# Two layers of attention and experts on one core: attention 1 without a barrier between its pairs, attention 2 entered batch by batch, two clearing blocks dropped

## The chip, the core and the metric

One core of a Trainium2 chip runs the whole program. The metric is the device time in microseconds, taken as the median of several runs.
## What is computed

`x` has 4 batches of 512 tokens, 256 wide, float32. Each of the four steps is a residual of the layer norm of `x`:

```python
x = x + attention_1(layernorm(x))        # one head, softmax(QK^T/16) V W_o inside each batch
x = x + experts_1(layernorm(x))          # 12 experts, top 3, 256 -> 640 -> 256, relu
x = x + attention_2(layernorm(x))        # 16 heads of 16, against 4096 given keys and values
x = x + experts_2(layernorm(x))          # 8 experts, top 2, and a shared one
```

Inside `experts_1` a token's result is the sum over its 3 experts, plus a bias row. That result of a whole batch is averaged over its tokens and goes through a small network, `phi = sigmoid(relu(pooled @ Wp1 + bp1) @ Wp2 + bp2)`; where `phi > 0.7` the batch's result is multiplied by 0.2. So a batch's `x` isn't known before all its expert rows are summed and averaged over tokens. For exactness attention 2 takes each row's maximum over 4096 scores before the exponentials.

## The kernel before

All of `x` stays in SBUF as 16 tiles of 128 tokens (4 a batch). There is no planner around the change: each engine's order is the order of its code in a block.

**Attention 1** (lines 314 to 518) works on two batches at a time, `lanes` one and two, each with 4 of the 8 PSUM banks and its own buffers. A `nc.Fori` loop of two rounds holds one block: layer norm 0 of both lanes (`norm_vector` on DVE, the power on POOL, transposes `norm_tensor` on PE, copies `norm_scalar` on ACT), `qkv`, `scores`, `turn_probs`, `weigh`, `output`, then `x` is updated (L506), layer norm 1, its rows written to DRAM (`normed_rows`, L350), and `router` (L429) gives the 12 logits. Each round ends with the block's end and `clear(...)` (L518), a second block in which the engines set 52 semaphores back to zero, since the loop body waits on constants.

**Experts 1** (to L927): routing on DVE, then 59 blocks of 128 token slots. Each block's result is written by POOL to the DRAM tensor `expert_rows`, by slot and expert rank. When all are written, SP reloads them (L644), 12 DMAs of 512 KB, 3 for each of the 4 batches, into the space of the second expert weights. DVE adds the three of a batch to `acc` (L922), and PE sums over tokens (L754). Then the block ends, and `clear` (L927) is a block again.

**Attention 2, first part** (L1072 to L1257) is one block. DVE works out all four batches' factors together (L1207 to L1221), updates batch 0's `x` (L1231) and normalises it; POOL updates the others (L1149, L1151). PE makes queries (`half_queries`, L1077), which are split in two float32r parts, written to DRAM (`store_queries`, L1102) and loaded back in the layout of the score products (`load_queries`, L1020). SP issues the loads of all keys first (L1003: the first quarter of the keys, then the rest), and batch 0's query store after them. Then come 64 units: PE makes a unit's scores (2 products of 128x512, L1042, `max_unit`) in one of two bank pairs, DVE reduces it to maxima (L1048). Unit `u` has query tile `u//16`, key block `u%16//2` and head pair `u%2`; the units from 4 on wait for the rest of the keys. Among the units `PIECE`, `STATS` and `APPLY` place the layer norm and the queries of batches 1 to 3, which PE does in lumps of half a batch. The next block (L1336) has the exponentials and weighted sums of attention 2, with further units among them.

Of the kernel before, what the change touches and what calls it, by code (L numbers as in the profile page):

```python
# [5 lines left out]
F32 = mybir.dt.float32  # L6
# [9 lines left out]
P = 128  # L16
# [36 lines left out]
def build(nc, a, out):  # L53
    with ExitStack() as ctx:
# [81 lines left out]
        class Lane:  # L136
            def __init__(self, tag, bank, xn, xnT, stack):
# [5 lines left out]
                self.stats_done, self.aggr_done, self.var_done, self.rstd_done, self.norm_done, self.turned, self.taken = self.norm_sems = (  # L143
                    [sem(n + tag) for n in ("ln_stats", "ln_aggr", "ln_var", "ln_rstd", "ln_norm", "ln_turned", "ln_taken")])
# [42 lines left out]
        main = Lane("", 0, xn, xnT, ctx)  # L187
# [44 lines left out]

        with ExitStack() as l0:
# [78 lines left out]

            with ExitStack() as at:
                scale = float(D) ** -0.5

                class AttnLane(Lane):
                    def __init__(self, c):
                        tag = str(c)
                        xn_, xnT_ = (xn, xnT) if c == 0 else (sb("xn1", [P, TB, D], F32, at), sb("xnT1", [P, KD, S], F32, at))  # L320
                        super().__init__(tag, 4 * c, xn_, xnT_, at)
# [5 lines left out]
                        self.nmax, self.rsum, self.rrec = (sb(n + tag, [P, TB], F32, at) for n in ("nmax", "rsum", "rrec"))  # L327
                        (self.q_mm, self.k_mm, self.v_mm, self.score_mm, self.pT_mm, self.pv_mm, self.proj_mm, self.route_mm,
                         self.q_taken, self.k_taken, self.v_taken, self.nmax_done, self.p_done, self.pT_act, self.pT_dve,
                         self.o_taken, self.rrec_done, self.x_done, self.rows_out) = self.attn_sems = sems(" ".join(n + tag for n in (  # L330
                             "q_mm k_mm v_mm score_mm pT_mm pv_mm proj_mm route_mm q_taken k_taken v_taken nmax_done "
                             "p_done pT_act pT_dve o_taken rrec_done x_done rows_out").split()))

                lanes = [AttnLane(c) for c in range(2)]
                assert NB % 2 == 0

                with nc.Fori(0, NB // 2) as b2i:
                    def rows_of(c):
                        return lambda t: x[:, bass.ds(2 * TB * b2i + TB * c + t, 1), :].rearrange("p o d -> p (o d)")

                    with nc.Block() as block:
                        @block.sync
                        def _(sp):
                            for j in range(E0 // 2):
                                e = bass.ds(E0 // 2 * b2i + j, 1)
                                sp.dma_start(w2all[:, e].rearrange("p o n d -> p (o n) d"),
                                             a["L0_ffn_w2"][e].rearrange("o (k p) i -> p (o k) i", p=P)).then_inc(w2_in, 16)
                            for c, L in enumerate(lanes):
                                sp.wait_ge(L.norm_done, 2 * TB)
                                sp.dma_start(normed.rearrange("(t p) d -> p t d", p=P)[:, bass.ds(2 * TB * b2i + TB * c, TB), :],  # L350
                                             L.xn[:]).then_inc(L.rows_out, 16)
                            for L in lanes:
                                sp.wait_ge(L.rows_out, 16)

                        @block.gpsimd
                        def _(pool):
                            for L in lanes:
                                norm_pool(pool, 0, L)
                            for L in lanes:
                                norm_pool(pool, 1, L)  # L360
                        @block.tensor
                        def _(pe):
                            def project(L, w, bank, done):
                                for m in range(KD):
                                    for k in range(KD):
                                        mm = nc.tensor.matmul(ps[:, bank + m, :], w[:, k, m * P:(m + 1) * P], L.xnT[:, k, :],
                                                              start=(k == 0), stop=(k == KD - 1))
                                    mm.then_inc(done, 1)

                            def qkv(L):  # L370
                                B = L.bank
                                pe.wait_ge(L.taken, KD)
                                pe.wait_ge(qkv_in, 16 * 3)
                                project(L, wq, B + 2, L.q_mm)
                                project(L, wk, B, L.k_mm)
                                for i in range(TB):
                                    if i % 2 == 0:
                                        pe.wait_ge(L.q_taken, i // 2 + 1)
                                    for k in range(KD):
                                        mm = nc.tensor.matmul(ps[:, B + 2 + i // 2, (i % 2) * D:(i % 2 + 1) * D],  # L380
                                                              L.xnT[:, k, i * P:(i + 1) * P], wv[:, k, :],
                                                              start=(k == 0), stop=(k == KD - 1))
                                    if i % 2:
                                        mm.then_inc(L.v_mm, 1)

                            def scores(L):

                                pe.wait_ge(L.k_taken, KD)
                                for i in range(TB):
                                    if i >= 2:  # L390
                                        pe.wait_ge(L.v_taken, i - 1)
                                    for m in range(KD):
                                        mm = nc.tensor.matmul(ps[:, L.bank + i, :], L.qT[:, m, i * P:(i + 1) * P], L.kT[:, m, :],
                                                              start=(m == 0), stop=(m == KD - 1))
                                    mm.then_inc(L.score_mm, 1)

                            def turn_probs(L):
                                pe.wait_ge(L.p_done, TB)
                                for kb in range(TB):
                                    for i in range(TB):  # L400
                                        mm = nc.tensor.transpose(ps[:, L.bank + kb, i * P:(i + 1) * P],
                                                                 L.pm[:, i, kb * P:(kb + 1) * P], ident[:])
                                    mm.then_inc(L.pT_mm, 1)

# [1733 lines left out]
```

## Time and profile before

| | us |
|---|---|
| median of 3 runs (lowest, highest) | 2159.94 (2159.7, 2162.9) |
| the profiled execution's own time | 2163.98 |
| its span, first to last instruction | 2162.3 |
| PE busy in the span | 1972.8 (91%) |
| DVE busy | 1555.3 (72%) |
| ACT busy | 1345.0 (62%) |
| POOL busy | 272.0 (13%) |

Durations below come from the one profiled execution, whose own time is 4.0 us above the median. In the timeline a row is: start in us, length in us, engine, line, operation, output<-inputs, count; in brackets how long the engine had been idle before and what ended that. PE ends are modelled. "PEq" or "issue" as a releaser stands for an engine's instruction queue, at block borders for the meeting of all engines.

### The profile page before, as it was taken

How to read it: one execution, taken by the hardware profiler on the slowest of the kernel's cores; microseconds unless marked ns; L12 is line 12 of the kernel's file. 1: busy time of each engine (PE TensorE's matmuls, PEld its weight loads, DVE VectorE, ACT ScalarE, POOL GpSimd, SP SyncE). 2: the span in 40 equal slices, each digit the busy share in tenths (PEclk: the TensorE clock that was granted, in tenths of full speed). 3: DMA queues.
4: the chain of work that ended last, by engine and by line, in shares of the span. 5: the costliest groups of instructions: out<-in, count | busy, mean ns of one | idle time of the engine just before them, and what ended most of it. 6: DMA issues, size and time to landing. Idle time of an engine off the chain costs nothing. (4 is left out here: it accounts for less than half of the span.)

```text
span 2162.3 us, 40151 instructions
## 1 busy us (share of the span) xinstructions
PE 1972.8 (91%) x15900; PEld 996.3 (46%) x15900; DVE 1555.3 (72%) x1956; ACT 1345.0 (62%) x2647; POOL 272.0 (13%) x280
## 2 busy tenths in 40 slices
PE   6793999996477999999999999999999999998995
PEld 3553889996222333333333333333333333446673
DVE  3436212223488999999999999999999999613454
ACT  1220444441012888888888888888888888784321
POOL 0000434431310000000000000000000000001473
PEclk9896899997566999999999999999999999999997
DMA  4201668874552311011310003201102000001135
GB/s 145 73 20 61 200 211 254 262 232 158 88 73 50 45 18 17 7 19 30 51 19 15 14 12 49 43 8 15 19 7 86 5 7 7 12 25 37 40 102 167
DMA packets 162028, 145.92 MB, mean 67 GB/s; under 512 B 85322, under 2 KB 132406, under 8 KB 161078
## 3 DMA queue, kind: packets, MB, share of 16 engines
q1 hardware_dynamic: 152438, 117.69, 22.2%
q0 software_dynamic: 9408, 25.70, 3.7%
q8 instruction: 126, 2.06, 0.4%
q14 instruction: 56, 0.46, 0.1%
HBM read 108.63 MB, written 32.10 MB: 65 GB/s over the span
## 5 line engine op out<-in xcount | busy, mean ns | idle before, releaser
L1048 DVE TENSOR_REDUCE maxp<-banks 128x2 f32<-128x1024 f32 x1024 | 1233.8, 1223 | 35.2 <-PE banks L1042 34.4
L1525 ACT ACTIVATE pring<-banks 128x512 f32<-128x512 f32 x2048 | 1107.3, 601 | 185.2 <-PE banks L1412 64.5
L1426 PE MATMUL banks<-pring,vcur 128*17 128x256 f32 x8192 | 637.9, 386 | 4.9 <-ACT osb L1519 4.0
L1412 PE MATMUL banks<-qst,kst 50*128 50x512 f32 x2048 | 510.9, 496 | 0.0
L1042 PE MATMUL banks<-kst,qst 50*128 50x512 f32 x2048 | 431.4, 419 | 28.3 <-DVE maxp L1048 25.5
L1412 PEld LDWEIGHTS banks<-qst,kst 50*128 50x128 f32 x2048 | 193.6, 184 | 425.8 <-ACT pring L1525 413.0
L1426 PEld LDWEIGHTS banks<-pring,vcur 128*17 128x17 f32 x8192 | 139.7, 95 | 370.5 <-issue 185.9
L1042 PEld LDWEIGHTS banks<-kst,qst 50*128 50x128 f32 x2048 | 199.7, 192 | 66.5 <-DVE maxp L1048 54.5
L773 ACT ACTIVATE hT<-banks,b 128x128 f32<-128x128 f32 x295 | 108.5, 368 | 187.8 <-PE banks L704 172.7
L911 DVE TENSOR_SCALAR yo<-banks,wblock 128x256 f32<-128x256 f32 x59 | 28.5, 483 | 224.5 <-PE banks L713 224.5
L1394 POOL TENSOR_TENSOR osb<-osb,bc 128x512 f32<-128x512 f32 x15 | 19.2, 1282 | 1169.2 <-DMA bc<-reciprocals 1169.2
L704 PE MATMUL banks<-xgT,w1r 128*128 128x128 f32 x1180 | 143.8, 278 | 1.0 <-issue 1.0
L704 PEld LDWEIGHTS banks<-xgT,w1r 128*128 128x128 f32 x1180 | 138.8, 195 | 1.4 <-issue 1.4
L713 PE MATMUL banks<-w2all,hT 128*128 x590 | 137.8, 381 | 0.0
L713 PEld LDWEIGHTS banks<-w2all,hT 128*128 128x128 f32 x590 | 107.6, 190 | 15.0 <-issue 2.7
L174 ACT COPY xnT<-banks 128x512 f32<-128x512 f32 x24 | 12.9, 589 | 109.9 <-PE banks L179 109.9
L657 POOL DMA_INDIRECT expert_rows<-yo,target_i x59 | 61.3, 1039 | 157.6 <-DVE yo L911 152.6
L179 PE MATMUL banks<-ident,xn 128*128 128x128 f32 x96 | 23.3, 387 | 63.3 <-DVE xn L160 42.9
L1822 PE MATMUL banks<-wgu,xgT 128*128 x156 | 52.5, 459 | 0.0
L169 POOL TENSOR_TENSOR rstd<-vareps,mhalf 128x4 f32<-128x4 f32 x16 | 16.2, 1016 | 260.7 <-DVE vareps L153 260.7
L179 PEld LDWEIGHTS banks<-ident,xn 128*128 128x128 f32 x96 | 14.5, 188 | 71.8 <-DVE xn L160 45.6
L2059 DVE COPY xgT<-banks 128x256 f32<-128x256 f32 x39 | 16.6, 425 | 36.7 <-PE banks L1835 36.7
(294 smaller groups left out, 1287.0 us busy)
## 6 DMA issues: line engine op xcount, KB each, us to landing
w1r<-in_L_ffn_w SPq DMA_DIRECT2D x59, 640.0 KB
kst<-key_parts SPq DMA_DIRECT2D x18, 512.0 KB
key_parts<-ksp SPq DMA_DIRECT2D x32, 256.0 KB, 3.4
w2all<-in_L_ffn_w SPq DMA_DIRECT2D x12, 640.0 KB, 7.5
w2all<-expert_rows SPq DMA_DIRECT2D x12, 512.0 KB, 8.7
qst<-query_parts SPq DMA_DIRECT2D x96, 64.0 KB
normed_rows<-xn SPq DMA_DIRECT2D x8, 512.0 KB, 2.9
kf<-in_kT SPq DMA_DIRECT2D x16, 256.0 KB, 5.7
```

Source lines behind the costliest of these rows:

```text
L179: mm = nc.tensor.transpose(ps[:, L.bank + k, t * P:(t + 1) * P], L.xn[:, t, k * P:(k + 1) * P], ident[:])
L657: nc.gpsimd.indirect_dma_start(placed, bass.IndirectOffsetOnAxis(ap=target_i[:, b:b + 1], axis=0), yo[b % YO][:], None).then_inc(y_out[b % ...
L704: mm = nc.tensor.matmul(ps[:, HB + n % HR, 0:P], w1r[b % W1R][:, k, i * P:(i + 1) * P], xgT[b % 2][:, k, :], start=(k == 0), stop=(k == KD ...
L713: mm = nc.tensor.matmul(ps[:, YB + b % 2, 0:D], hT[b % 2][:, i, :], w2all[:, bass.ds(e, 1), i, :].rearrange("p o d -> p (o d)"), start=(i ...
L773: nc.scalar.activation(hT[b % 2][:, i, :], ps[:, HB + n % HR, 0:P], ACT.Relu, bias=b1[:, bass.ds(e * NI + i, 1)]).then_inc(h_taken, 1)
L911: nc.vector.tensor_scalar(yo[b % YO][:], ps[:, YB + b % 2, 0:D], wblock[:, b:b + 1], None, ALU.mult).then_inc(y_taken, 1)
L1042: mm = nc.tensor.matmul(ps[:, base + r, :], qst[i][rows, hp, qt * P:(qt + 1) * P], keys[rows, hp, kb * 512:(kb + 1) * 512], start=True, st ...
L1048: return nc.vector.tensor_reduce(maxp[:, :, hp, qt, kb], ps[:, base:base + 2, :], X, ALU.max)
L1412: nc.tensor.matmul(ps[:, score_bank(n), :], kst[g % 2][rows, j // 2, kt * P:(kt + 1) * P], qst[i][rows, j // 2, :], start=True, stop=True) ...
L1426: mm = nc.tensor.matmul(ps[32 * j:32 * j + VC, 7, cols], vcur[g % 2][:, kt, j, :], pring[:, (G % 2) * HG + j, cols], start=(kt == 0 and ha ...
L1525: nc.scalar.activation(pring[:, n % (2 * HG), :], ps[:, score_bank(n), :], ACT.Exp, scale=float(DH) ** -0.5).then_inc(exp_done, 1)
L1822: mm = nc.tensor.matmul(ps[:, bank, 0:2 * H1], xgT[b % 2][:, k, :], wgu[:, k, bass.ds(experts[b], 1)].rearrange("p o g h -> p (o g h)"), s ...
```

## The change

It has three parts.

**Attention 1.** The loop is written out, in one block, and semaphores count on instead of being cleared. The second layer norm of a lane is an object of its own, `L.late`, whose rows and transposes lie in the lane's probabilities `pm`. The second pair's first layer norm is placed before the first pair's `add_result`; the first pair's transposes (`turn_late`) and router products come after the second pair's `qkv`.

**Clearing.** `clear` is no longer called after attention 1 and after experts 1. ACT sets attention 1's 68 semaphores back in the experts' block, after its second exponential, and the experts' 29 in attention 2's first block.

**Attention 2, first part.** The expert rows are reloaded in this block, batch 0's three DMAs first, then the first quarter of the keys, then batches 1 to 3, into `kst[1]`, `pring` and a new buffer. DVE adds batch 0's and 1's rows, POOL 2's and 3's. The factor is worked out for batch 0, for batch 1, and for 2 and 3 together among the units. The rest of the keys is loaded after batch 0's queries, and units go by key block first, so that only those from 16 on need it. POOL normalises batches 1 to 3. PE makes queries in single pieces of two instructions, and the token sums of batches 2 and 3 at units 2 to 5 and 8 to 11.

```diff
-                with nc.Fori(0, NB // 2) as b2i:
-                    with nc.Block() as block:
-                    clear(*[s for L in lanes for s in L.norm_sems + L.attn_sems])
+                with nc.Block() as block:
...
+                        for it in range(PAIRS_OF_BATCHES):          # PE
+                            qkv(one, it)
+                            qkv(two, it)
+                            if it:
+                                for L in lanes:
+                                    turn_late(L, it - 1)
+                                for L in lanes:
+                                    router(L, it - 1)
+                            scores(one, it)
+                            scores(two, it)
+                            turn_probs(one, it)
+                            turn_probs(two, it)
+                            weigh(one, it, 0)
+                            weigh(one, it, 1)
+                            weigh(two, it, 0)
+                            output(one, it)
+                            weigh(two, it, 1)
+                            if it + 1 < PAIRS_OF_BATCHES:
+                                norm_tensor(pe, it + 1, one)
+                            output(two, it)
+                            if it + 1 < PAIRS_OF_BATCHES:
+                                norm_tensor(pe, it + 1, two)
...
+                            if it + 1 < PAIRS_OF_BATCHES:           # DVE, after the softmax sums
+                                dve.wait_ge(x_loaded[1], 16)
+                                for c, L in enumerate(lanes):
+                                    norm_vector(dve, it + 1, rows_of(it + 1, c), L)
                             for c, L in enumerate(lanes):
+                                add_result(c, it)
+                                dve.wait_ge(L.pT_mm, TB * (it + 1))
+                                norm_vector(dve, it, rows_of(it, c), L.late)
...
-                clear(step, sums_done, *route0_sems, *fill_sems, *block_sems, *xg_in, *w1_in, *y_out, *sums_in)
...
+                PIECE = {u0 + i if i < TB else u1 + i - TB: (b, i) for b, u0, u1 in ((1, 6, 23), (2, 32, 38), (3, 47, 53))
+                         for i in range(TB + KD * KD)}
+                def first_unit(n):
+                    kb, qt, h = n // 8, n % 8 // 2, n % 2
+                    return 16 * qt + 2 * kb + h
...
+                        load_sums(sp, 0)                            # SP
                         sp.wait_ge(zeros_set, 1)
+                        load_zeros(sp, 0)
                         load_ones(sp, 0, keys_in0)
                         load_keys(sp, 0, 0, keys_in0, slice(0, FEW))
+                        for c in range(1, NB):
+                            load_sums(sp, c)
+                        store_half(sp, 0, 0)
+                        sp.wait_ge(q_stored, 16)
+                        load_query_parts(sp, 0, 0)
                         load_keys(sp, 0, 0, keys_in1, slice(FEW, KEYS))
+                        store_half(sp, 0, 1)
...
+                        pow_of(0)                                   # POOL
+                        for n, c in enumerate((2, 3)):
+                            pool.wait_ge(erows_in[c], 16 * TOP0)
+                            for k in range(TOP0):
+                                w = nc.gpsimd.tensor_tensor(acc[:, tiles, :], acc[:, tiles, :], expert_sums[c][:, k], ALU.add)
                         for b in range(1, NB):
+                            pow_of(b)
+                            for t in range(TB * b, TB * (b + 1)):
+                                nc.gpsimd.tensor_scalar(xn[:, t - TB * b, :], x[:, t, :], meanvar[:, t, 0:1], rstd[:, t:t + 1],
+                                                        ALU.subtract, ALU.mult).then_inc(main.norm_done, 1)
+                            for m in range(KD):
+                                leave(pool, b, m)
...
+                        add_rows(0)                                 # DVE
+                        factors(0, 0, 1, 2)
+                        residual(0, 0)
+                        stats_of(0)
+                        (normalise batch 0)
+                        add_rows(1)
                         (split batch 0's queries, as before)
+                        factors(1, 1, 2, 6)
+                        residual(1, 1)
                         stats_of(1)
                         for u in range(NU):
+                            if u in FACTOR:
+                                factor_step(FACTOR[u], 2, 2, NB, POOLED_BANK)
+                            if u in LATE:
+                                residual(LATE[u], 2)
+                                stats_of(LATE[u])
                             dve.wait_ge(max_mm, u + 1)
+                            max_reduce(first_unit(u), 0, 4 + 2 * (u % 2)).then_inc(max_taken, 1)
```

`add_rows` is two additions of 128x1024 and four of 128x256, `factors` the eight steps of L1207 to L1221 for one batch, `residual` one operation of 128x1024. On PE the token sums of batch 0 come before its transposes, those of batch 1 (16 instructions) after batch 0's queries. `FACTOR` puts the eight steps of batches 2 and 3 at units 12 to 25, `LATE` their residual and statistics at 26 and 28.

## Rows read from the trace of the kernel before

**Rows 1.** The page, busy tenths of DVE in 40 slices.
```profile
DVE  3436212223488999999999999999999999613454
```

**Rows 2.** Timeline of PE in attention 1.
```profile
33.67 3.60 PE L366 MATMUL banks<-xnT,wq 128*128 128x512 f32 x8
43.99 13.90 PE L393 MATMUL banks<-kT,qT 128*128 128x512 f32 x32
...
82.87 1.04 PE L179 MATMUL banks<-ident,xn 128*128 128x128 f32 x8
88.84 6.82 PE L429 MATMUL banks<-wr,xnT 128*128 128x12 f32 x32
...
129.39 13.90 PE L393 MATMUL banks<-kT,qT 128*128 128x512 f32 x32
```

**Rows 3.** Timeline of DVE around the two rounds of attention 1.
```profile
73.59 0.88 DVE L506 SCALAR_TENSOR_TENSOR x<-banks,rrec,x 128x256 f32 x2 [11.77 <-PE banks L419]
...
183.35 0.35 DVE L205 TENSOR_REDUCE zmax<-z 128x16 f32<-128x192 f32 x1 [1.87 <-PEq L97]
```

**Rows 4.** Busy times, mean granted clock, DMA share and GB/s: the router products.
```profile
88.84:95.80 6.96, 6.82 (x34) 6.72 (x32) 0.21 (x1) 1.07 (x2) 0.00 (x0) 0.50 0.22 75
```

**Rows 5.** Timeline at a block border without a clearing block.
```profile
675.81 0.21 DVE L1069 STREAM_TRANSPOSE mrows<-mparts 128x32 f32<-128x32 f32 x1
676.31 0.61 SPq L1027 DMA_DIRECT2D maxima<-mrows  x1
```

**Rows 6.** Timelines of SP, DVE and PE from the last expert row to the units.
```profile
513.10 13.83 SPq L644 DMA_DIRECT2D w2all<-expert_rows  x12
521.07 3.74 DVE L922 TENSOR_TENSOR acc<-acc,w2all 128x1024 f32<-128x1024 f32 x3 [10.82 <-DMA w2all<-expert_rows]
543.20 0.17 DVE L1207 TENSOR_SCALAR pooled<-banks 128x8 f32<-128x8 f32 x1 [5.16 <-PEq L97]
546.96 1.67 DVE L1231 SCALAR_TENSOR_TENSOR x<-acc,fac,x 128x256 f32<-128x256 f32 x4
551.85 2.85 DVE L160 TENSOR_SCALAR xn<-x,meanvar,rstd 128x256 f32<-128x256 f32 x4 [1.16 <-POOL rstd L169]
556.81 5.22 PE L1077 MATMUL banks<-xnT,wqt 128*128 128x512 f32 x8 [1.16 <-ACT xnT L174]
560.35 0.69 DVE L1238 CAST qsp<-banks 128x512 fp32r<-128x512 f32 x1 [5.65 <-PE banks L1077]
561.85 0.38 SPq L1102 DMA_DIRECT2D query_parts<-qsp  x1
577.00 1.25 SPq L1020 DMA_DIRECT2D qst<-query_parts  x3
583.80 6.39 DVE L1048 TENSOR_REDUCE maxp<-banks 128x2 f32<-128x1024 f32 x5 [14.29 <-PE banks L1042]
```

**Rows 7.** DMA queue from 554 to 577 (packets, MB, share); landing of the query stores.
```profile
q1 hardware_dynamic: 550, 2.72, 92.5%
...
DMA to landing us min/median/max: 2.8/2.8/15.1
```

**Rows 8.** The line of the unit reductions, 583.8 to 675.08, idle before the first included.
```profile
L1048 DVE TENSOR_REDUCE maxp<-banks 128x2 f32<-128x1024 f32 x64 | 74.2, 1217 | 25.2 <-PE banks L1042 24.4
```

**Rows 9.** Timeline of PE among the units: a transposed tile, a unit, a lump.
```profile
612.87 0.69 PE L179 MATMUL banks<-ident,xn 128*128 128x128 f32 x2
613.49 0.79 PE L1042 MATMUL banks<-kst,qst 50*128 50x512 f32 x2
616.33 3.78 PE L1077 MATMUL banks<-xnT,wqt 128*128 128x512 f32 x4
```

**Rows 10.** POOL's additions (whole span); normalising on DVE beside POOL's work, and alone.
```profile
L1151 POOL TENSOR_TENSOR x<-x,acc 128x1024 f32<-128x1024 f32 x3 | 7.0, 2341 | 0.2
...
552.86 1.20 DVE L160 TENSOR_SCALAR xn<-x,meanvar,rstd 128x256 f32<-128x256 f32 x1
608.25 1.37 DVE L160 TENSOR_SCALAR xn<-x,meanvar,rstd 128x256 f32<-128x256 f32 x4
```

More of the change, by code:

```diff
@@ L582, in build @@
                 GROUPS = TOP0
-                spent = w2all[:].rearrange("p e n d -> p (e n) d")
-                sums = [spent[:, c * TOP0 * TB:(c + 1) * TOP0 * TB].rearrange("p (k t) d -> p k t d", k=TOP0) for c in range(NB)]
                 def key_load(n):
@@ L1167, in _, with pool_tokens @@
[L1167 to L1169 removed]
+                        def pool_tokens(c, i, bank):
+                            if c < 2:
+                                pe.wait_ge(erows_done, TB * c + i + 1)
+                            else:
+                                pe.wait_ge(rows_added, c - 1)
+                            for m in range(KD):
+                                mm = nc.tensor.matmul(ps[:, bank + m, c:c + 1], acc[:, TB * c + i, m * P:(m + 1) * P],
+                                                      ones[:, 0:1], start=(i == 0), stop=(i == TB - 1))
+                            return mm
@@ L1233, in _, with add_rows @@
-                        ch.wait()
-                        stats_of(0)
-                        apply_of(0)
+                        ch = Chain(dve, steps[0])
+                        def add_rows(c):
+                            tiles = slice(TB * c, TB * (c + 1))
+                            dve.wait_ge(erows_in[c], 16 * TOP0)
+                            for k in range(TOP0 - 1):
+                                ch(nc.vector.tensor_tensor(acc[:, tiles, :], acc[:, tiles, :], expert_sums[c][:, k], ALU.add))
+                                ch.wait()
+                            for i in range(TB):
+                                t = TB * c + i
+                                nc.vector.tensor_tensor(acc[:, t, :], acc[:, t, :], expert_sums[c][:, TOP0 - 1, i], ALU.add
+                                                        ).then_inc(erows_done, 1)
@@ new lines, in factors, with residual @@
+                        def factors(n, c0, c1, bank):
+                            for i in range(8):
+                                factor_step(i, n, c0, c1, bank)
+                        def residual(b, n):
+                            tiles = slice(TB * b, TB * (b + 1))
+                            dve.wait_ge(fac_done, n + 1)
+                            ch(nc.vector.scalar_tensor_tensor(out=x[:, tiles, :], in0=acc[:, tiles, :], scalar=fac[:, b:b + 1],
+                                                              in1=x[:, tiles, :], op0=ALU.mult, op1=ALU.add))
+                            ch.wait()
```

595 lines of the change are left out of this document (334 added, 261 removed).

## The prediction, made before the changed kernel was run

> **What bounds the kernel now.** I read the page first, the 40 slices before anything else, then the timelines of the stages that the diff touches, engine by engine, and last the waits inside them. From slice 14 on DVE is at nine tenths or more [rows 1]; that long stretch is the softmax of attention 2 and isn't touched. So the change can only pay in what lies before: attention 1 (to 181.5 us), the border to the experts, and the stretch from the last expert row (513) to the last of the 64 units (675). All of these are serial chains; a microsecond taken off them is a microsecond of the end, since the stage behind starts only when all engines have met.
>
> In attention 1 PE is the chain: it works without a gap up to the second layer norm, and then the second round's scores start at 129.39, 85.40 after the first round's at 43.99 [rows 2]. Between, PE waits for layer norms and runs the router products at the half level, 0.50 [rows 2, 4]. DVE meanwhile had stood idle for 11.77 us ahead of L506 [rows 3].
>
> From 513 on the chain is DMA, DVE, PE, DMA, DVE: reload, additions, factor, normalisation, queries, their way through DRAM, first maximum at 583.80 after 14.29 us of idle DVE [rows 6]. Then DVE is the bound of the units, with 74.2 us of reductions [rows 8].
>
> **Part 1, attention 1.** The second pair's first layer norm moves into the idle 11.77 us of DVE: two lanes at some 4.4 us are 8.9, so it fits and costs nothing; had it not that cover, it would delay L506 by the excess. Its transposes take PE about 0.9 us a lane (8 in 1.04, the last one's tail left out [rows 2]), the first lane's ahead of `output(two)`, where PE waited 0.7 us anyway. The last `output` ended at 82.9, so both lanes are turned at about 84.1. `qkv` of both: 2 x (43.99 - 33.67 = 10.32) = 20.6, to 104.7. The late transposes are 1.8, the wait for ACT's first copy 0.4, to 106.9. The 32 router instructions took 6.82 at 0.50 [rows 2, 4]; PE comes to them now from 80 us of dense work, so I take them at the full level, half of that, 3.4: scores at 110.3. Against 129.39 that is **19.1 us**. If the clock had fallen it would be 15.7; without any wait for ACT 19.5. DVE's late layer norm runs beside `qkv` and ends before the first key copy. The second half of the w2 loads is issued behind the row stores and has a hundred microseconds. The end of the last pair (transposes, router, logits) stays as it was.
>
> **Part 2, clearing.** The border to the experts costs 1.87 us from the last logits to the next DVE work [rows 3]; a border without a clearing block costs 676.31 - 676.02 = 0.3 [rows 5]. So **1.6 us**, between 1 and 1.9. The second clearing lies in part 3's chain. The clears on ACT are 68 and 29 in a row: the old block did 13 an engine inside 1.9 us, so at most 0.15 each, 10 and 4 us, and ACT had nothing to do there for over 30 us either time. Without that idle time they would be on the path in full.
>
> **Part 3a, up to the first unit.** SP reloads from 513.10 as before, and batch 0's three DMAs came first before too: additions from 521.07, no gain. Two of 1.25 and four small ones in 1.67 end at 525.2. The 16 token sums start with the first tile, at 0.22 each at half clock (router rate), so they end at 527.7. The old chain from L1207 to L1231 is 546.96 - 543.20 = 3.76: `x` can be worked on at 531.5. Residual 1.3, statistics 2.0, POOL's power 1.2: 536.0. Normalising took 2.85 beside POOL's work [rows 6]; POOL has now nothing to do yet, and alone it is 1.4 [rows 10]. Then PE turns tiles at half clock (2.5, overlapped by half a microsecond), ACT copies 1.1, queries from about 540.2. From their start to the first DVE split it was 560.35 - 556.81 = 3.5, to the second 5.3: 543.7 and 545.5. The first half is stored at 545.2 (561.85 - 560.35 = 1.5 after).
>
> Is DVE free then, and the queue? Their additions began 4.4 us after one another before, so a batch takes the queue 4.4 us. Ahead of batches 1 to 3 stand now the ones and a quarter of the keys, 0.92 MB at 2.72 MB in 23 us [rows 7], 7.8 us. So batch 1 lands near 535.5, 2 at 540, 3 at 544.5. `add_rows(1)` takes DVE from 537.5 to 541.5: hidden. The store meets an empty queue. Before, it stood behind 3.1 MB of keys, and 15.1 us passed until the loads of 577.00; the median from issue to landing is 2.8 [rows 7]. So: loads from 548.2, landed like the old ones (583.80 minus a unit minus 577.00, less two zero loads) at 552.3. This is what the reordering is worth: about 12 us of DMA and, above, 17 us of three batches that needn't be waited for.
>
> DVE goes on: second half's split to 546.9, batch 1's token sums on PE to 547.3, factor 3.8, residual 1.3, statistics 2.0: first maximum near **554.5**, against 583.80, **29.3 us**. Here DVE, no longer the query loads, is last. Bounds: each of some 12 DVE operations after 540 beside POOL's additions may cost 0 to 0.8 us (1.20 against 1.37 / 4 = 0.34 alone [rows 10]), so 554 to 561.
>
> A rule stands against this. The Trainium skill, SBUF — State Buffer (section Who interferes with whom), says that DVE with two SBUF inputs and a GpSimd operation that reads SBUF exclude each other for a whole instruction. The row beside it disagrees in degree: a DVE operation of 1.20 us began at 552.86 and ended within one of POOL that ran from 552.69 to 555.65. By the rule in full, my sum would lose what the first rival has, by rows.
>
> **Part 3b, the 64 units.** Old: 91.3 from first to last, of it 74.2 reductions, 6.7 layer norm of two batches, 25.2 - 14.3 = 10.9 idle. New: reductions 74.2. The normalising is off DVE (-2.7), residual (2 x 1.3) and eight factor steps (1.6) are on: 8.2 in all. Idle time grows, since PE gets more and in a worse place. At half clock a unit takes PE about 0.73, a turned tile 0.62, a piece 3.71 / 2 = 1.85 [rows 9], and DVE 1.14 a unit. Four pieces in four units make 2.6 each, 1.45 over DVE: 5.8 a batch for batches 2 and 3; for batch 1 the steps of units 23 to 25 and the 3.3 us at unit 26 hide part, 3.9. The lumps before left DVE idle 3.3 a batch, because two of them let the clock rise. Token sums at 0.9 in units 2 to 11: 3. Turned tiles: 0.25 x 8 = 2. Together 20.5. Sum 74.2 + 8.2 + 20.5 = 103, against 91.3: **+11.6**. If the clock rises early (it did within 7 to 10 us of dense PE work), the idle is no more than before and this is +2; if every wait adds, +16. The rest of the keys, 2.36 MB from 551, needs 20 us to 573, and unit 16 is due at 576: hidden by 3 us, and otherwise a wait of its own.
>
> The last maximum comes then at 554.5 + 103 = 657.5 in the old scale, 17.7 earlier. POOL's normalising of batch 1 follows its additions (6 x 2.34 from 540, to 554.5) and ends near 559, before the turned tiles of unit 6.
>
> **Sum.** 19.1 + 1.6 + 29.3 - 11.6 = 38.4 us. From the profiled execution's own 2163.98 this gives 2125.6; that one is 4.0 above the median of 2159.94, so I forecast **2121.5**. Its own range, from the bounds above (gains of 15.7 to 19.5, 1 to 1.9, 23 to 30, costs 2 to 16): a loss of all at once isn't likely, 2111 to 2133.
>
> **Rivals.**
> 1. *POOL and DVE exclude each other.* POOL's six additions of 2.34 us [rows 10] lie from 540 to 554, on just the DVE chain that is last. DVE gets in only between them: factor and residual of batch 1 end when POOL's do, first maximum 558 to 559, and POOL, delayed as well, normalises batch 1 only by 562 to 565, where PE, in order, stands before unit 6. 6 to 10 us: 2129. For it: the stretched rows at 551.85 and 552.86. Against it: none was stretched to the end of POOL's instruction. 17 in 100.
> 2. *The clock comes up early among the units.* PE is loaded densely from unit 2 on, and each stretch of extra work lifts the clock before its end; the idle stays at 11 and the stage costs 2 instead of 11.6: 2112. For it: old second lumps. Against it: stretches of 10 us, as long as the rise took. 15.
> 3. *The queries of batch 0 still wait.* If SP or the rings hold the store until batches 1 to 3 and half of the keys are through, the 12 us come back, and unit 16 waits too: 2136. Against it: by amounts the ring is empty in time. 7.
> 4. *Slower than before: instruction supply.* The written-out attention 1 has every instruction once, with no loop, and a stream must be fetched. One stall of POOL for "issue", 5.0 us at 491, is in the trace. Were PE to stand so at each stage of attention 1 and at each border, from the eighth stall on the gain is gone: 2165. Against it: the rest of the kernel is written out and PE shows no such stall in 2000 us. 3.
> 5. *It doesn't do what it says*: the stages gain, and the softmax starts no sooner because something else (value or query loads of the next block) is last: within 0.2%, 2160. 3.
>
> The forecast keeps 55. Eight in ten lie between **2108 and 2137**. Faster by over 0.2% (4.3 us, about what the measurement can tell): 0.94; within: 0.03; slower: 0.03.
>
> **What would show it.** Scores of the second pair near 110 with the clock at 1.0 in the router; a border of 0.3 us ahead of `zmax`; all routing times earlier by 20.7. From the last expert row to the first unit 41.4 us in place of 70.7; the query store landing in under 4 us; DVE's L1048 with idle time near 20 inside the stage. Wrong would be a DVE operation of over 1.5 us beside POOL, PE waiting for `xn` at unit 6 or for keys at unit 16, and ACT's clears ending later than the first relu.

## The result, and the profile after

The changed kernel took 2128.59 us (median of 4 runs, 2126.09 to 2131.45) against 2160.34 for the kernel before beside it: ratio 0.9851, 95% interval [0.9834, 0.9869], 31.8 us. Forecast were 2121.5 and 38.4. Two further sets of runs gave 0.9851 [0.9837, 0.9864] and 0.9852 [0.9837, 0.9867], so the size is firm and the forecast was some 7 us too good. The profiled execution has its own time of 2126.49 and a span of 2124.7; that of before, 2163.98 and 2162.3. Between these two lie 37.6 us of span, more than between the medians; why, is the last point of the explanation.

The page's rows of DVE's busy tenths, of TensorE's granted clock and the line of the unit reductions over the whole span, where [rows 1] had DVE's:

```profile
DVE  2537112224889999999999999999999999513454
PEclk9995999997568999999999999999999999999997
L1095 DVE TENSOR_REDUCE maxp<-banks 128x2 f32<-128x1024 f32 x1024 | 1235.4, 1224 | 20.9 <-PE banks L1089 19.9
```

The nine tenths begin with slice 13 and are as even as before: the softmax wasn't touched, what is gained lies ahead of it. PE in attention 1 (columns of a timeline: start, busy us, engine, line, operation, count, idle before and who ended it), to be held against [rows 2]:

```profile
104.81 1.91 PE L180 MATMUL banks<-ident,pm 128*128 128x128 f32 x16
107.01 3.74 PE L454 MATMUL banks<-wr,pm 128*128 128x12 f32 x32 [0.29 <-ACT pm L175]
110.60 15.68 PE L411 MATMUL banks<-kT,qT 128*128 128x512 f32 x32
126.11 3.72 PE L419 MATMUL banks<-ident,pm 128*128 128x128 f32 x32
```

The second pair's scores start at 110.60 (forecast 110.3, before 129.39), but they take 15.68 where the same 32 products took 13.90. The windows of the same stretch (window, length, busy PE, granted clock, DMA share, GB/s) name the reason; 0.50 is the lower of the two levels, 1.2 GHz:

```profile
107.01:110.75 3.74, 3.74 (x33) 0.99 0.00 0
111.00:114.00 3.00, 3.00 (x4) 0.50 0.00 0
114.30:128.00 13.70, 13.70 (x45) 1.00 0.01 2
```

Here the router ran at full clock, as I took it; the fall came behind it, in the scores, with PE busy all the time. It is part of the change: all eight profiles with both routers ahead of both scores have such a stretch at 0.50, from 109 to 112 us on, 3.4 us long in four of them and 6.8 us in the other four, where it begins inside the router (4.13 to 4.52 us in place of 3.74). DVE at the border to the experts, where [rows 3] has 1.87:

```profile
164.62 0.21 DVE L532 TENSOR_TENSOR z<-banks,br 128x48 f32<-128x48 f32 x1 [3.21 <-PE banks L454]
165.16 0.35 DVE L206 TENSOR_REDUCE zmax<-z 128x16 f32<-128x192 f32 x1 [0.33 <-PEq L349]
```

Routing starts 18.2 us earlier (forecast 20.7), and the border is 0.33 as read off a border without a clearing block [rows 5]. Then DVE from the last expert row to the first unit, against [rows 6]:

```profile
503.36 2.48 DVE L1344 TENSOR_TENSOR acc<-acc,kst 128x1024 f32<-128x1024 f32 x2 [10.97 <-DMA kst<-expert_rows]
505.88 1.43 DVE L1348 TENSOR_TENSOR acc<-acc,kst 128x256 f32<-128x256 f32 x4
...
518.14 1.38 DVE L1406 TENSOR_SCALAR xn<-x,meanvar,rstd 128x256 f32<-128x256 f32 x4 [1.16 <-POOL rstd L1223]
519.44 4.55 DVE L1344 TENSOR_TENSOR acc<-acc,kst 128x1024 f32<-128x1024 f32 x2
524.03 9.90 DVE L1348 TENSOR_TENSOR acc<-acc,kst 128x256 f32<-128x256 f32 x4
533.85 0.68 DVE L1411 CAST qsp<-banks 128x512 fp32r<-128x512 f32 x1
...
543.49 3.49 DVE L1095 TENSOR_REDUCE maxp<-banks 128x2 f32<-128x1024 f32 x3
```

The same six additions take 3.9 us for batch 0 and 14.4 for batch 1 (12.4 in the two later profiles of this kernel): four small ones of 0.36 each take 2.5 each. A DVE operation of over 1.5 us beside POOL was one of the signs of being wrong that the prediction named. POOL at that time, and the DMA queue behind the split:

```profile
520.57 8.11 POOL L1232 TENSOR_TENSOR acc<-acc,pring 128x1024 f32<-128x1024 f32 x3 [2.46 <-DMA pring<-expert_rows]
528.64 7.49 POOL L1232 TENSOR_TENSOR acc<-acc,last_rows 128x1024 f32<-128x1024 f32 x3
```
```profile
535.34 0.37 SPq L1177 DMA_DIRECT2D query_parts<-qsp  x1
538.09 2.65 SPq L1060 DMA_DIRECT2D qst<-query_parts  x6
```

POOL's six additions take 2.5 to 2.7 us each, and DVE's wait for one each. The store lands in 2.75 us. From the last scatter (492.67; 510.53 before) to the first maximum are 50.8 us where there were 73.3: 22.4 gained of 29.3. Last, the line of the 64 units from 543.4 to 639.4, against [rows 8]:

```profile
L1095 DVE TENSOR_REDUCE maxp<-banks 128x2 f32<-128x1024 f32 x64 | 75.8, 1221 | 12.7 <-PE banks L1089 11.7
```

The stage lasts 95.9 us, 4.6 more than before, where I had added 11.6.

### The profile page after: what moved, and what is told of

Read it like the earlier page. It is cut to its first block and busy times, and to the rows that moved or that the text cites. A ratio compares the mean times of both kernels' runs of the same rounds, so it can differ in the third digit from the quotient of the medians.

```text
span 2124.7 us, 40040 instructions
## 1 busy us (share of the span) xinstructions
PE 1971.0 (93%) x15912; PEld 997.2 (47%) x15912; DVE 1559.4 (73%) x1960; ACT 1343.0 (63%) x2648; POOL 287.5 (14%) x292
## 3 DMA queue, kind: packets, MB, share of 16 engines
q1 hardware_dynamic: 152438, 117.69, 22.4%
## 5 line engine op out<-in xcount | busy, mean ns | idle before, releaser
L1095 DVE TENSOR_REDUCE maxp<-banks 128x2 f32<-128x1024 f32 x1024 | 1235.4, 1224 | 20.9 <-PE banks L1089 19.9
L711 POOL DMA_INDIRECT expert_rows<-yo,target_i x59 | 61.3, 1039 | 158.0 <-DVE yo L960 153.0
L175 ACT COPY xnT<-banks 128x512 f32<-128x512 f32 x16 | 8.6, 589 | 62.5 <-PE banks L180 62.5
L1913 POOL DMA_INDIRECT expert_rows<-yo,target_i x39 | 38.5, 987 | 23.0 <-ACT yo L2095 14.8
L2038 PE MATMUL banks<-wd,hT 88*128 x156 | 40.4, 381 | 1.2 <-DVE hT L2248 1.2
L1907 POOL DMA_INDIRECT xg<-normed_rows,source_i x39 | 38.2, 981 | 11.8 <-issue 9.9
```

The lines of the kernel that those rows point to most:

```text
L711: nc.gpsimd.indirect_dma_start(placed, bass.IndirectOffsetOnAxis(ap=target_i[:, b:b + 1], axis=0), yo[b % YO][:], None).then_inc(y_out[b % ...
L1095: return nc.vector.tensor_reduce(maxp[:, :, hp, qt, kb], ps[:, base:base + 2, :], X, ALU.max)
L2038: mm = nc.tensor.matmul(ps[:, 5 + u % 2, 0:D], hT[u % 2][0:HC, c, :], wd[:, bass.ds(e, 1), c, :].rearrange("p o d -> p (o d)"), start=(c = ...
```

## The experiments

Four kernels ran together, beside the kernel before (2162.19 us there).

**The changed kernel again.**

> The changed kernel itself, timed again beside the kernel before, as the reference for the other runs on this chip. If the 31.8 us measured so far are the change's own, the median difference is 31 to 33 us; if the two groups of its four runs (2126 and 2131) are two phases of the clock that a run falls into, both groups come again, and in the profile the stretch to 640 us is the same in either, with the difference behind it.

2131.7 us (2126.43 to 2133.06), ratio 0.9851. The stretch to 640 was not the same: here the first maximum stands at 542.47, a microsecond earlier than in the first profile, and the last ends at 642.55, 3.2 later. So the expected split into two groups, equal up to 640, is not what came: the runs lie between 2126 and 2133 us, and the difference is made inside the units as well as behind them.

**The clearing blocks put back.**

> The changed kernel with its two clearing blocks put back (behind attention 1, and behind the expert block, with ScalarE's clearing inside the blocks taken out). Theory: each costs one barrier round: z to zmax goes from 0.33 back to about 1.9 us of idle, and the expert border gains 1 to 1.5 us, so 2 to 3 us slower than the changed kernel. Rival: the second one is hidden behind the last scatter's landing (VectorE waits 10.97 us for the reloaded rows anyway), then only 1.5 us.

```
+                clear(*attn1_used)          # behind attention 1
-                        for s in attn1_used:
-                            act.sem_clear(s)
-                        for s in block0_used:
-                            act.sem_clear(s)
+                clear(*block0_used)         # behind the expert block
```

2134.3 us (2133.03 to 2137.51), ratio 0.9868 [0.9853, 0.9883] against 0.9851 [0.9837, 0.9864]: about 3.7 us slower, 2.6 between the medians, and the intervals overlap, so that the times alone don't settle it. Its rows at the two borders:

```profile
168.14 0.35 DVE L206 TENSOR_REDUCE zmax<-z 128x16 f32<-128x192 f32 x1 [2.06 <-PEq L97]
...
499.73 0.14 POOL L1215 MEMSET zeros<- 2x64 f32 x1 [4.05 <-POOLq L97]
```

2.06 against 0.33, and 4.05 against 2.77 in the changed kernel: 1.7 and 1.3. The second isn't hidden: the reload is issued after the border, so DVE's wait for it moves along. From the last scatter (494.71) to the first addition (506.73) this kernel takes 12.0 us, the changed kernel 10.6 to 10.7.

**POOL's additions left out.**

> GpSimd's six additions of the expert rows of batches 2 and 3 are left out (those rows are not added; all signals remain). Lock theory (VectorE and GpSimd exclude each other for a whole instruction where both read two operands from SBUF): VectorE's additions of batch 1 fall from 14.4 us to the 3.9 that the same six take for batch 0, the first maximum starts at about 535 instead of 543.5, and the kernel is 8 to 9 us faster than the changed one. Rival (VectorE is slow there because the rows are still landing, or the store and reload of the queries are the bound): the additions stay above 10 us, or the first maximum stays within 1.5 us of 543.5.

```
-                                w = nc.gpsimd.tensor_tensor(acc[:, tiles, :], acc[:, tiles, :], expert_sums[c][:, k], ALU.add)
+                            nc.gpsimd.memset(pool_spare[:, n:n + 1], 0.0).then_inc(rows_added, 1)
```

DVE in this kernel:

```profile
521.62 2.48 DVE L1340 TENSOR_TENSOR acc<-acc,kst 128x1024 f32<-128x1024 f32 x2
524.14 1.43 DVE L1344 TENSOR_TENSOR acc<-acc,kst 128x256 f32<-128x256 f32 x4
527.75 0.69 DVE L1407 CAST qsp<-banks 128x512 fp32r<-128x512 f32 x1 [2.17 <-PE banks L1155]
...
530.66 0.69 DVE L1407 CAST qsp<-banks 128x512 fp32r<-128x512 f32 x1 [1.50 <-PE banks L1155]
```

With nothing on POOL the additions of batch 1 take 3.9 us, exactly those of batch 0, though the same rows are loaded: the lock theory holds, and the rival of late rows falls. Of the 10.5 us only 5 to 7 arrive at the first maximum (33.3 us behind the first addition; 40.1, 38.2 and 38.1 in the three profiles of the changed kernel), since DVE now waits for the queries, which PE computes at half clock (8 products in 6.70 us), 2.17 and 1.50. Median 2126.54 (2125.64 to 2129.44), 5.2 under the changed kernel's 2131.7, where 8 to 9 were expected.

**Router and scores lane by lane.**

> TensorE in attention 1's second pair: router of lane one, scores of lane one, router of lane two, scores of lane two, in place of both routers ahead of both scores; VectorE takes the logits of lane two behind the row maxima of lane one. Theory (the granted clock fell to 0.50 at 111 to 114 us because 16 transposes and 32 narrow products stood in one stretch): with half of them together the clock stays up, the scores take 13.9 us again and the pair ends 1.8 us earlier. Rival (the dip is a late answer to the idle time ahead of it, or any such group is enough): the dip stays, no change within 0.5 us, or it comes twice.

```
-                                for L in lanes:
-                                    router(L, it - 1)
-                            scores(one, it)
-                            scores(two, it)
+                            for L in lanes:
+                                if it:
+                                    router(L, it - 1)
+                                scores(L, it)
```

PE, and the windows:

```profile
107.01 1.96 PE L454 MATMUL banks<-wr,pm 128*128 128x12 f32 x16 [0.29 <-ACT pm L175]
108.82 7.11 PE L411 MATMUL banks<-kT,qT 128*128 128x512 f32 x16
115.77 1.85 PE L454 MATMUL banks<-wr,pm 128*128 128x12 f32 x16
117.47 7.11 PE L411 MATMUL banks<-kT,qT 128*128 128x512 f32 x16
```
```profile
107.01:109.00 1.99, 1.99 (x17) 1.00 0.00 0
111.00:114.00 3.00, 3.00 (x8) 1.00 0.01 3
```

No fall, and the last logits at 162.72 in place of 164.62: 1.9 us, as the theory had it. The median is 2128.9 (2125.66 to 2132.48), inside the changed kernel's range. But this is one profile. Four later ones have the same order; in one of them the clock stays up too, in three it falls again for 3.4 us, as in the kernel 'both' below:

```profile
108.03 8.81 PE L411 MATMUL banks<-kT,qT 128*128 128x512 f32 x16
```
```profile
109.00:112.00 3.00, 3.00 (x5) 0.50 0.02 5
```

From the router's start to the scores' end are 17.6 us without a stretch at 0.50, 19.3 with one of 3.4 us, and 20.9 with one of 6.8 us. The last logits come at 162.7 to 163.3 in the five profiles with the new order and at 164.6 to 166.2 in the eight with the old one. So the order gains some 2 us because the stretch at half clock is shorter or absent; that it is always absent, as the theory had it, doesn't hold.

The second four ran beside 2163.83 us.

**Attention 1 alone changed.**

> The kernel before with attention 1 alone changed (both pairs in one block without the barrier between them; the clearing behind it and everything from the expert block on as before). Theory: it carries 16.7 to 17 us of the 31 (z of the last lane moved from 181.27 to 164.62 in the changed kernel, and the clearing's 1.5 us are not in it), so about 2144 against 2161. Rival: the earlier start of the expert block is taken back by its loads (it would wait for weights), and less than 12 us are left.

2149.94 us (2147.83 to 2151.09), ratio 0.9937 [0.9923, 0.995]: 13.9 us, between theory and rival. The profile shows the stages where the theory has them: last logits at 164.89, and the block behind the units starts at 657.89 in place of 676.35, 18.5 earlier (16.4 of it at the last logits, 2.0 in shorter units). What is given back is given back later: the table below.

**The old order of the units.**

> The changed kernel with the 64 maximum units in the order of the kernel before (query tile by query tile), so that the wait for the second part of the keys falls ahead of unit 4 in place of unit 16. The keys are issued at 540.8 to 543.5 and the DMA engines are full until about 561; theory: units 4 and on wait until 560 to 562, 10 to 12 us slower. Rival (VectorE, busy 1.13 us a unit with work of batches 2 and 3 between, has the slack to catch up): under 4 us slower.

```
-                    return 16 * qt + 2 * kb + h
+                    return n
-                            if u == 2 * KEYS // 512:
+                            if u == 4:
```

```profile
545.58 0.80 PE L1089 MATMUL banks<-kst,qst 50*128 50x512 f32 x2
546.30 1.01 PE L1252 MATMUL banks<-ones,acc 128*128 128x1 f32 x4
562.38 0.80 PE L1089 MATMUL banks<-kst,qst 50*128 50x512 f32 x2 [15.07 <-DMA kst<-key_parts]
```

One wait of 15.07 us; the median is 2146.39 us (2140.86 to 2147.7) and the ratio 0.9913 [0.9895, 0.993] against 0.9851, 13.4 us slower. So with the loads in their new order, the order of the units is worth over 40% of the whole gain: it is what lets most of the keys come after the queries. In the changed kernel PE doesn't wait at unit 16.

**POOL's additions moved beside the units.**

> GpSimd adds the expert rows of batches 2 and 3 behind the normalisation of batch 1, beside the maximum units, in place of ahead of it, and what follows from them moves 8 units later (the pooled sums stand in bank 0). Lock theory: VectorE's additions of batch 1 take 3.9 us; GpSimd's additions run at 2.3 to 2.6 us each beside row maxima, which read from PSUM, and slow them by nothing; the first maximum comes 33 us behind the first addition of batch 0 (38 to 40 in the changed kernel), 5 to 7 us of it kept, less 1 to 3 us for the last batch's queries at the end of the block. Rival (the exclusion holds for every pair of instructions of the two engines): the maxima beside the additions grow from 1.15 to over 2 us each and the gain is gone.

```
+                            if b == 1:
+                                add_last_rows(pool)      # was ahead of pow_of(1)
-                POOLED, POOLED_BANK = {2: 2, 3: 8}, 2
+                POOLED, POOLED_BANK = {2: 12, 3: 16}, 0
-                FAC_AT = 12
+                FAC_AT = 20
-   ((1, 6, 23), (2, 32, 38), (3, 47, 53))
+   ((1, 6, 23), (2, 40, 44), (3, 54, 58))
```

2128.26 us, ratio 0.9835 [0.9822, 0.9849]. DVE's additions take 3.9 us, the first maximum is at 538.13, 33.1 us behind the first addition. The units run to 638.78, 100.7 us. By the ratios that is 3.5 us under the changed kernel, with intervals that still overlap.

**This and the lanes' order together.**

> adds_in_units and routers_split together. If the two gains are independent, 1.9 us in attention 1 and 3 to 6 us at the units: 2122 to 2126 us, ratio to the kernel before 0.981 to 0.984. If the clock's rise behind the units (16 to 27 us behind the start of the next block in the profiles so far) goes by how much TensorE did ahead of it, part of it is taken back: each of those microseconds more costs about 0.45.

2126.46 us (2124.38 to 2127.74; 2122 to 2126 were expected), ratio 0.9829 [0.9815, 0.9842]. POOL and DVE beside one another:

```profile
540.77 7.22 POOL L1232 TENSOR_TENSOR acc<-acc,pring 128x1024 f32<-128x1024 f32 x3
547.93 7.21 POOL L1232 TENSOR_TENSOR acc<-acc,last_rows 128x1024 f32<-128x1024 f32 x3
```
```profile
534.65 15.49 DVE L1095 TENSOR_REDUCE maxp<-banks 128x2 f32<-128x1024 f32 x13
```

13 maxima in 15.5 us, 1.19 each, the last eight of them beside POOL's additions of 2.4 us: no exclusion where DVE reads PSUM. The first maximum is at 534.65, 8.8 earlier than in the changed kernel's first profile, but the last one ends at 635.9, only 3.5 earlier.

**Filling TensorE's gaps.** As PE's work among the units is mostly at half clock, two kernels tried to keep the clock up.

> 'both', and each of the 32 maximum units that has no piece of a later batch and no pooled sum beside it is computed twice into the same bank (same result), so that TensorE stands idle nowhere among the 64 units. Theory (the clock falls to 0.50 among the units and stays there behind them because TensorE is idle a third of each bare unit): the granted clock is 1.00 in more of the stretch and at the start of the next block; the pieces' waits (17 to 18 us of VectorE's idle time) shrink by half or more, the rise behind the block comes under 10 us in, and the kernel is 5 to 12 us faster than 'both'. Rival: the clock doesn't answer to these products; each doubled unit takes 1.6 us in place of 1.13, 10 to 15 us slower.

```
+                            if u not in PIECE and not 12 <= u < 20:
+                                max_unit(first_unit(u), 0, kst[0], 4 + 2 * (u % 2))
                             max_unit(first_unit(u), 0, kst[0], 4 + 2 * (u % 2)).then_inc(max_mm, 1)
```

2125.42 us (ratio 0.9817, beside 2165.4). Neither theory: it costs nothing that can be seen and gives nothing that can be told from 'both'. Its windows:

```profile
540.00:546.00 6.00, 6.00 (x20) 0.50 1.06 123
558.00:564.00 6.00, 6.00 (x24) 0.50 0.00 0
570.00:576.00 6.00, 6.00 (x16) 0.73 0.00 0
```

PE is busy without a gap in these windows, and the clock stays at 0.50; it rises at 573.2, behind 6.6 us of units and query pieces (128 rows by 512 columns) without a gap.

> As gaps_doubled, but all 64 units are computed twice. Theory: the clock stays at 1.00 from some 15 to 25 us into the stretch, where a doubled unit takes 0.9 to 1.0 us and is hidden under VectorE's 1.13; about the same as 'both' or up to 8 us faster. Rival (the clock doesn't answer): TensorE needs 1.6 us for each and its pieces on top, the stretch grows from 101 to 135 us or more.

The edit is the same without the condition. 2136.04 us, ratio 0.9872 [0.985, 0.9895], 9.6 above 'both' by medians, units to 646 in place of 636: the clock doesn't stay up for these either. The stage takes 111 us, where the rival had 135 or more; a likely reason, not tested, is that part of the doubling falls where PE waited.

**Both, and the changed kernel, again.**

> 'both' once more, on the same chip as the changed kernel. If its gain is its own and not the scatter of the clock's phase, it is 2 to 6 us faster than after_third, with medians 2124 to 2128 beside 2127 to 2132; if the clock's phase decides, the two medians lie within 1 us.

> The changed kernel a third time, beside both_again. 2127 to 2132 us and 31 to 33 us under the kernel before; the runs between 2126 and 2133 again, since the 64 units take 96 to 101 us and the clock's rise comes 16 to 27 us into the next block.

2126.17 us (2123.29 to 2127.53) and 2131.26 (2128.54 to 2132.83), beside 2163.88: 5.1 us, ranges that don't touch. So 'both' is faster than the changed kernel; against the kernel before its ratio is 0.9826 [0.9812, 0.9839].

## Why the prediction was right or wrong

**Attention 1: 19.1 forecast, 16.7 measured** (15.1 to 16.7 over the eight profiles). Each step to the scores held: 106.9 for the router, 3.4 for it (3.74), 110.3 for the scores (110.60). The step that failed is the one not written down, that the scores' 13.90 stay 13.90. Placed behind transposes and 12-column products, they ran at half clock for 3.4 us and lost 1.8; in the four profiles with 6.8 us at half clock, router and scores together lost 3.4. Changing the lanes' order shortens that stretch, but it is still there in three of five profiles. I looked for the clock in the router and not in what follows it.

**Clearing: 1.6 forecast; 1.5 in the profiles (1.87 to 0.33).** The second clearing I left inside the chain of part 3a, without a term; the kernel that puts both back shows 1.3 for it. Right in size and reason by these rows; in the times it is hardly clear of the scatter.

**To the first unit: 29.3 forecast, 22.4 measured.** The sum's sentence that failed is "`add_rows(1)` takes DVE from 537.5 to 541.5: hidden". It took 14.4 us in place of 4. I had bounded DVE's stretching beside POOL by one row of 1.20 us, and laid POOL's additions beside twelve small operations of the wrong stretch, 540 and later. They began as soon as their rows had landed, 17.2 us behind the first addition where I had 19, and fell on the additions of batch 1; even by my own figures the two overlapped from 540 to 541.5. This is rival 1, to which I gave 17 in 100, in mechanism though not in place: it costs DVE's additions, not the factor chain. Its time, 2129, is the one measured, and its 6 to 10 us are the 6.9 lost here; that the total agrees so well is luck, since the other terms were off as well. The Trainium skill's rule (SBUF — State Buffer, Who interferes with whom) was right in full and my reading of the row beside it wrong: the four additions of 0.36 us took one POOL instruction each, 2.5. The two kernels with POOL's additions gone or moved settle it, with 3.9 us each. The row of 552.86 [rows 10] was no witness against it: that operation reads one wide operand and two columns, not two wide ones, so it isn't of the kind that I had quoted the rule for; what stretched it, no run asks. To weigh a rule, the row must show the same operands.

A part of the loss was cover for something else. Without the lock DVE waits 3.7 us for the queries, so of 10.5 us of stretching 5 to 7 were the price. The 33.3 us from the first addition to the first maximum in the kernel without POOL's additions are the 33.4 that the forecast had (521.07 to 554.5): the rest of the chain was right.

In detail: normalising 1.38 (1.4 forecast), and the store landing in 2.75, so that rival 3 didn't come. No run put the store back behind the keys, so "about 12 us of DMA" is not shown as such; the old order of the units, where unit 4 waits 15.07, shows that late keys pay only with units that ask for them late.

**The units: +11.6 forecast, +4.6, +8.8 and +6.6 measured** (95.9, 100.1 and 97.9 us in the three profiles; 91.3 before). Reductions were nearly right at 75.8. The idle time was forecast at 20.5 and is 12.7, 17.2 and 14.9: the term that was mis-sized. I had every query piece at half clock, 1.85, 22.2 us for the 24 products; in each batch of four the clock rises in the second piece in the first profile, in the third or fourth in the second, and the 24 products take 17.9, 21.4 and 20.4 us. In the trace of before they had taken 17.7. Rival 2 had this mechanism and overdid it. So two errors, 7 us too good up to the first unit and 3 to 7 too bad behind it, nearly met. That is luck: had the units cost 11.6 us as forecast, the time would have come to 2131 to 2136, near the upper end of the range.

**The end: 1 to 5 us that no term had.** In all fourteen profiles the block behind the units starts at half clock, and the clock rises some time into it. From some 10 us in, PE has no idle time there (5.00 of 5.00 us busy from 650 to 655, at 0.50), so that stretch goes by the clock. Eight of them, with the block's start, the rise, and the span:

| kernel | block starts | clock rises | between | start to mark | mark to end | span less start |
|---|---|---|---|---|---|---|
| before | 676.35 | 696.4 | 20.1 | 1183.0 | 302.9 | 1485.9 |
| changed | 640.63 | 656.8 | 16.2 | 1181.3 | 302.8 | 1484.1 |
| changed, again | 643.82 | 661.5 | 17.7 | 1182.0 | 304.1 | 1486.1 |
| changed, third | 640.78 | 660.5 | 19.7 | 1183.0 | 303.0 | 1486.0 |
| POOL's additions out | 636.63 | 663.1 | 26.5 | 1186.0 | 305.0 | 1491.0 |
| clearing put back | 646.00 | 672.6 | 26.6 | 1185.8 | 304.0 | 1489.8 |
| attention 1 alone | 657.89 | 684.4 | 26.5 | 1185.9 | 302.6 | 1488.5 |
| both | 637.69 | 651.7 | 14.0 | 1180.4 | 306.1 | 1486.5 |

The mark is the last row of `mneg<-maxp` on DVE, close to the end of the softmax. Three rows behind the table, of the changed kernel: the block's first product, the window in which the clock rises, and the mark.

```profile
640.63 1.22 PE L1089 MATMUL banks<-kst,qst 50*128 50x512 f32 x4 [2.71 <-PEq L1180]
```
```profile
656.00:657.00 1.00, 1.00 (x10) 0.60 1.24 262
```
```profile
1821.96 0.28 DVE L1099 TENSOR_REDUCE mneg<-maxp 128x16 f32<-128x128 f32 x1
```

Up to the mark the time follows the rise in all fourteen profiles: from 1180.4 us where it comes after 14.0, through 1182.0 to 1182.3 where it comes after 17.7 to 18.2, to 1185.8 to 1186.0 where it comes after 26.5, about 0.45 us for each microsecond at half clock. Behind the mark another 302.5 to 306.1 us follow, which don't go by that rise; there the granted clock falls to 0.50 several more times, for 37 to 48 us together, and the profile of 'both' has the most of it and the longest time. Where the rise comes 26.5 us in, the whole remainder is 1488.5 to 1491.0; in the eleven others 1484.1 to 1487.9. The late rise is how attention 1 alone lost 2.5 of its 18.5 us by the end of the span. It is also why the spans of before and changed lie 37.6 us apart and their last maxima only 35.7: the rise of before comes 3.9 us later, which is 1.7 us. My sum of 38.4, met to 3 to 6 us at the last maximum (35.7, 32.5 and 35.6 earlier), says little on a median. The profile of before was also a slower execution than the four timed beside the first result (2163.98 against 2159.7 to 2162.9), the changed one's first (2126.49) one of its fastest (2126.09 to 2133.06 over 13 runs). What sets the moment of the rise was not found: filling PE's gaps among the units left it at 16.1 and 17.9. Of the other rivals, 4 and 5 didn't come: PE shows no wait for "issue" in attention 1, and the softmax starts 35.7 us sooner.

## What to carry to other kernels

Before work goes to a second engine "in parallel", look at the operands of what the first does meanwhile: two engines that both read two operands from SBUF take turns by whole instructions, so that the smaller instruction pays, and four small pieces pay four times. Put such work beside operations that read PSUM. Where loads feed a loop, reorder the loop so that its first part needs the data that is small and first, and store what is on the chain before the rest; without the loop's new order 13.4 of the 31.8 us were gone.

Look for a fallen clock behind a stretch of small products too, not only in it. A gain that ends ahead of a stretch at half clock is known to a few microseconds only, so compare at a border of stages first, and at the median second.

## What was not expected of the hardware

- PE's granted clock fell to 0.50 for 3.4 or 6.8 us in or behind 16 transposes and 32 products of 12 columns, with PE busy but for 0.3 us, in all eight profiles with this order. With 16 of the 32 behind wide products it fell for 3.4 us in three profiles of five, and not at all in two.
- In the kernel with the gaps filled, pairs of products of 50 rows by 512 columns, with token sums of one column between, kept PE busy for 17.9 of 18 us (546 to 564), and the granted clock was 0.50 throughout; the next rise came among the query pieces (570 to 576, 0.73).
- In the second profile of the changed kernel the two wide additions of batch 1 began ahead of POOL's and ran at 1.24 us each; the four small ones, of 0.36 alone, took 2.48 each. POOL's three beside them took 8.08, the next three 7.43: the price falls nearly all on the engine whose instructions are short.
